# An attention and expert kernel: down products three chunks behind, a third buffer for middle values, other places for loads and last results

## The reference, cut to what matters

```python
x = x + xattn(layernorm(x), ctx, ...)          # x is (8, 256, 256), ctx (8, 77, 256); differential attention, 16 heads
x = x + ffn(layernorm(x), gate_w, gate_up_proj, down_proj)

def ffn(hidden_states, gate_w, gate_up_proj, down_proj):      # E = 8 experts, I = 1024, TOP_K = 2
    x = hidden_states.reshape(-1, H)                          # 2048 tokens x 256
    probs = softmax(x @ gate_w.T)
    w, idx = top_k(probs, TOP_K)
    w = w / sum(w, axis=-1, keepdims=True)
    combine = zeros((T, E)).at[arange(T)[:, None], idx].add(w)
    def step(acc, (gup, dn, ce)):
        g, u = split(x @ gup.T, 2, axis=-1)
        return acc + ce[:, None] * (silu(g) * u @ dn.T)
    return scan(step, zeros_like(x), (gate_up_proj, down_proj, combine.T))
```

## Time and profile before

| | |
|---|---|
| device time, median of 3 runs | 564.85 us (564.73 to 565.91) |
| time of the profiled execution | 568.35 us |
| its span, first to last instruction | 566.5 us |
| TensorE busy (products) | 499.4 us, 88% |
| VectorE, ScalarE, GpSimd busy | 385.6, 339.0, 273.6 us (68%, 60%, 48%) |
| mean granted TensorE clock | 0.946 of 2.4 GHz |
| up products, 1440 | 188.8 us busy |
| down products, 720 | 104.3 us busy |

### The profile page before, as it was taken

The page is one execution under the profiler, slowest core; times in us unless marked ns, Lnnn a source line. Parts: engine busy times, 40 slices in busy tenths (PEclk is TensorE's granted clock), DMA queues, the critical chain, the costliest instruction groups (busy, mean ns, idle before and its releaser), DMA issues.

```text
span 566.5 us, 12111 instructions
## 1 busy us (share of the span) xinstructions
PE 499.4 (88%) x3738; PEld 367.4 (65%) x3756; DVE 385.6 (68%) x805; ACT 339.0 (60%) x642; POOL 273.6 (48%) x347
## 2 busy tenths in 40 slices
PE   4695889999998888689798999999999999999970
PEld 3463556676665655325576888878888888777640
DVE  5337358889887747587577988887676676666551
ACT  1220488889789777275575777765665556554530
POOL 5006454575554544104126565656567566563244
PEclk9986699999999989699899999999999999999985
DMA  6567757768667543463646767866555545563133
GB/s 215 189 162 163 233 144 239 209 190 249 218 170 216 171 132 95 137 200 113 172 103 112 151 131 196 183 116 153 91 104 85 96 76 94 100 71 65 20 32 43
DMA packets 88090, 79.89 MB, mean 141 GB/s; under 512 B 49176, under 2 KB 73368, under 8 KB 87896
## 3 DMA queue, kind: packets, MB, share of 16 engines
q1 hardware_dynamic: 76512, 63.38, 40.7%
q0 software_dynamic: 11520, 15.74, 17.1%
HBM read 49.08 MB, written 22.41 MB: 126 GB/s over the span
## 4 chain that ended last, share of the span: by engine, by line
PE 65%; DMA 9%; DVE 7%; ACT 7%; issue 6%; SPq 2%; POOL 2%; another core or an unknown queue 1%; ACTq 0%; DVEq 0%; POOLq 0%
PE bank L1441 25%; PE bank L1458 12%; PE bank L1270 5%; PE bank L1224 5%; PE bank L1256 4%; DVE FB L1156 2%; PE bank L1293 2%; DVE FB L1160 2%; PE bank L1470 2%; PE bank L1306 2%; PE bank L1238 2%; PE bank L1279 2%; ACT FB L867 2%; DMA x_parts<-WE 2%; PE bank L1318 2%
## 5 line engine op out<-in xcount | busy, mean ns | idle before, releaser
L1441 PE MATMUL bank<-FB,WE 128*128 128x0 bf16 x1440 | 188.8, 281 | 2.7 <-DVE FB L1156 1.0
L1441 PEld LDWEIGHTS bank<-FB,WE 128*128 x1440 | 137.4, 98 | 34.9 <-issue 5.1
L700 POOL DMA_INDIRECT out<-FB,slot_tok x60 | 100.4, 1674 | 97.7 <-DVE FB L1172 93.3
L867 ACT ACTIVATE FB<-FB 128x512 bf16<-128x512 f32 x120 | 75.6, 630 | 71.1 <-DVE FB L1156 63.2
L1160 DVE TENSOR_TENSOR FB<-FB 128x512 bf16<-128x512 f32 x120 | 83.3, 694 | 47.4 <-ACT FB L867 42.2
L1458 PE MATMUL bank<-FB,WE 128*128 128x0 bf16 x720 | 104.3, 281 | 5.3 <-DVE FB L1160 3.3
L1156 DVE TENSOR_TENSOR FB<-FB,bank 128x512 f32<-128x512 f32 x120 | 82.0, 683 | 28.8 <-ACT FB L861 22.3
L691 POOL DMA_INDIRECT FB<-x_parts,slot_tok x60 | 61.2, 1020 | 69.0 <-DVE slot_tok L1124 27.0
L861 ACT ACTIVATE FB<-bank 128x512 f32<-128x512 f32 x120 | 70.6, 588 | 34.0 <-PE bank L1441 28.3
L1458 PEld LDWEIGHTS bank<-FB,WE 128*128 x720 | 68.1, 98 | 23.9 <-issue 8.3
L624 POOL TENSOR_TENSOR WE<-FB,WE 128x256 bf16<-128x256 f32 x104 | 67.9, 679 | 23.0 <-ACT WE L731 23.0
(11 more groups left out here) (180 smaller groups left out, 618.9 us busy)
## 6 DMA issues: line engine op xcount, KB each, us to landing
FB<-w SPq DMA_DIRECT2D x26, 512.0 KB, 5.5
WE<-w SPq DMA_DIRECT2D x44, 256.0 KB
WE<-q_parts SPq DMA_DIRECT2D x32, 200.0 KB
WE<-x SPq DMA_DIRECT2D x16, 256.0 KB, 5.3
q_parts<-FB SPq DMA_DIRECT2D x32, 128.0 KB
x_parts<-WE SPq DMA_DIRECT2D x20, 128.0 KB, 4.3
out<-WE SPq DMA_DIRECT2D x20, 128.0 KB, 5.3
q_parts<-WE SPq DMA_DIRECT2D x16, 128.0 KB
```

Of the source, the lines that this page charges most:

```text
L700: pool.indirect_dma_start(out=out, out_offset=bass.IndirectOffsetOnAxis(ap=slot_tok[:, c:c + 1].bitcast(U32), axis=0), in_=y_sb[c % 2], in ...
L867: nc.scalar.activation(hT[k % 3][:, 0, :], hid[k % 2], ACT.Copy).then_inc(hi_ready, 1)
L1441: ins = nc.tensor.matmul(to, wf[:, bass.ds(at + o, P)], xgT[s % 2][:, 2 * part + kc, :].shape_from_register(long[s % 2]), start=(z == 0), ...
```

## The change

It does these things:

- The down products of a chunk come after the up products of the third chunk behind it (`LAG = 3`), and three, not two, are left after the last up. The results of a slot are turned back after chunk 4 and chunk 7 of the next slot (chunk 5 in the last slot).
- ScalarE does silu(k) before hidden_hi(k - 1), VectorE hidden(k) before hidden_lo(k - 1). In slots 0 to 3 (k < 32) a third buffer, `hid_more`, in the place of weights that come later, joins the two of `hid`, and silu(k) waits for hidden_lo(k - 3).
- The late parts are split at other chunks (`FILL_OF`); the results are scaled at chunks 5, 6 of the next slot and 0, 1 of the one after.
- On SP the loads of late parts of a slot's last two chunks stand behind the first turns of the following slot; the last x load stands before the first four late loads.
- X2 of tile 15 stands before LG of tile 14.
- Of the last eight result tiles the first two go to `y_sb` as before, then two to free parts of `xgT`, two to `xg` and two to `y_sb`; two of the last four turned halves have banks of their own, and a semaphore `y_end` counts four of the last scatters.

```diff
+FILL_OF = ((3, 4, 5, 7), (4,), (2, 3, 4, 7), (2, 3, 4, 7), (1, 2, 3, 4, 5, 6, 7), (1, 2, 3, 4, 5, 6, 7))
...
+LAST = NTP - SUB
+LAG = 3
+THREE = EARLY * FC
...
+        hid_more = tail[:, 2 * W1N - 2 * CAP:2 * W1N].bitcast(F32)
...
+        def hid_of(k):
+
+            return (*hid, hid_more)[k % 3] if k < THREE else hid[k % 2]
+
+        def turned_bank(n):
+
+            return {2 * NS - 3: y_bank(NS - 2, 1), 2 * NS - 1: bank[0]}.get(n, turn_bank)
...
+        def result_tile(c):
+
+            if LAST - 2 <= c < LAST:
+                return xgT[NS % 2][:, c % 2, :].bitcast(F32)
+            return xg[c % 2].bitcast(F32) if LAST <= c < LAST + 2 else y_sb[c % 2]
...
-                if kind == "OO" and TPB * b + i == TT - TPB - 2:
+                if kind == "XD" and b == B - 1:
                     for j in range(LSTG):
                         load_late(j)
...
-                        if FC * s + (0, 3)[half] <= due[j] < FC * s + (3, FC)[half]:
+                        if FC * s + (-2, 3)[half] <= due[j] < FC * s + (3, FC - 2)[half]:
                             load_late(j)
...
                     for p in range(2):
-                        pool.wait_ge(y_out[p], 8 * c)
+                        pool.wait_ge(y_out[p], 8 * c - 16 * (c == LAST))
+                if c == LAST:
+                    pool.wait_ge(y_end, 32)
...
             def silu(k):
                 act.wait_ge(g_mm, k + 1)
-                if k >= 2:
-                    act.wait_ge(lo_ready, k - 1)
-                nc.scalar.activation(hid[k % 2], up_bank[k % 2][0][:, :], ACT.Silu).then_inc(sil_ready, 1)
+                if k >= (3 if k < THREE else 2):
+                    act.wait_ge(lo_ready, k - (2 if k < THREE else 1))
+                nc.scalar.activation(hid_of(k), up_bank[k % 2][0][:, :], ACT.Silu).then_inc(sil_ready, 1)
...
+                    silu(k)
                     if k > 0:
                         hidden_hi(k - 1)
-                    silu(k)
-                    if c in (1, 2) and s > 0:
-                        yT_copy(s - 1, c - 1)
+                    if c in (2, 3) and s > 0:
+                        yT_copy(s - 1, c - 2)
...
-                if c >= 2:
+                if LAST <= c < LAST + 2:
+                    dve.wait_ge(xg_turned[c % 2], 32 * (NS - 1))
+                elif c >= LAST + 2:
+                    dve.wait_ge(y_out[c % 2], 16 * (c // 2 - 2))
+                elif LAST - 2 <= c < LAST:
+                    dve.wait_ge(g_mm, FC * (NS - 1))
+                elif c >= 2:
                     dve.wait_ge(y_out[c % 2], 16 * (c // 2))
...
+                    hidden(k)
                     if k > 0:
                         hidden_lo(k - 1)
-                    hidden(k)
-                    if c in (4, 5, 7) and s > 0:
-                        result(SUB * (s - 1) + (4, 5, 7).index(c))
-                    if c == 0 and s > 1:
-                        result(SUB * (s - 1) - 1)
+                    if c in (5, 6) and 0 < s < NS - 1:
+                        result(SUB * (s - 1) + c - 5)
+                    if c in (0, 1) and s > 1:
+                        result(SUB * (s - 2) + 2 + c)
+                    if c in (5, 6) and s == NS - 1:
+                        result(SUB * (s - 1) + 2 * (c - 5))
+                        result(SUB * (s - 1) + 2 * (c - 5) + 1)
...
-                    if c >= 2:
-                        down(s, c - 2, at[s])
+                    if c >= LAG:
+                        down(s, c - LAG, at[s])
                     elif s > 0:
-                        down(s - 1, FC - 2 + c, at[s - 1])
-                    if c in (3, 6) and s > 0:
-                        turned_result(s - 1, c // 6)
+                        down(s - 1, FC - LAG + c, at[s - 1])
+                    if c == 4 and s > 0:
+                        turned_result(s - 1, 0)
+                    if c == (7 if s < NS - 1 else 5) and s > 0:
+                        turned_result(s - 1, 1)
```

31 lines of the change are left out of this document (17 added, 14 removed).

## The result

The changed kernel takes 559.8 us (median of four runs, 558.9 to 560.6) where the kernel before took 565.4 beside it (564.7 to 568.5): a ratio of 0.989, 95% interval 0.985 to 0.993. It is faster by 5.6 us; the forecast had 16.2 us and a range that ended 5 us short of the time. The profiled execution has a span of 558.5 us in a time of 560.4, against 566.5 us in the earlier trace rows. So the two profiles are 8.0 us apart where the medians are 5.6 us apart: the profiled execution of the kernel before was itself a long one, 568.35 us.

The account below looks back on a forecast made before the run. TensorE, the busiest engine, was taken to bound the kernel, with gapless products from slot 4 on. Terms 2.35 + 9.8 - 0.9 + 0 + 4.9 = 16.15 us took 564.85 to 548.6 us; range 545.5 to 554.5 us.

Parts of the forecast that it names:

- all three stretches: Slots 0 to 3, the end of attention and the tail: where TensorE's products do not follow each other without a gap.
- Part 3: Slots 4 to 13, two hid buffers: ring of 1.96 us stays under TensorE's 2.335; 0 us, bounds -0.5 and +2.
- Part 2: Slots 0 to 3: new order and third buffer open the ring, 9.8 us gained; 0.9 us taken off for late rows.
- Rival A: Slots 1 to 3: turned rows become the bound, lengths stay; 4.2 us less gain, 552.8 us; chance 0.18.
- The one named above all: Sign that the forecast is wrong: the stretches before slot 4 shorten by less than 6 us together.
- the ring: Slots 0 to 3: hidden, hidden_hi, hidden_lo and hops make 1.99 us a chunk, costing 0.43 us where products need 1.56.
- Part 1: End of attention: x sooner (1.70) and two swapped products (0.65) start the expert stage 2.35 us sooner; ends 0 and 3.1.
- Rival C: End of attention and turns: clock stays up after the shorter wait, no turn is late; 546.5 us; chance 0.10.
- Part 4: Tail: one down chunk sooner (0.9 us) and last results in their own homes (4.0 us), together 4.9 us.
- D: Slots 0 to 3: the 1.99 us ring closes again over hT or up banks; 556.5 us; chance 0.04.
- E: Slots 4 to 14: two buffers make one serial ring, 2.58 us a chunk against 2.335; 570 us; chance 0.04.
- B: End of attention: x lands sooner but another transfer or the clock holds; 2.35 us less, 551.0 us; chance 0.12.

Follow-up runs that it names:

- i_res: The changed kernel with plain copies for turns and only the order of the results put back: 553.4 us, ratio 0.987 to the kernel before.
- k_res: The same kernel as i_res (only the order of the results put back), run again on another visit: 554.3 us, ratio 0.984.
- the control: The kernel before with each of its 56 turns replaced by two plain copies of half the bytes, turning left out: 565.5 us, ratio 0.998.
- j_tail_only: The kernel before with plain copies for turns and only the last results in eight homes: 563.7 us, ratio 0.997.
- h_after: The changed kernel with its turns replaced by plain copies, nothing else altered: 560.3 us, ratio 0.991 to the kernel before.
- i_two_buf: The changed kernel with plain copies for turns and without the third middle-value buffer, two in every slot: 564.2 us, ratio 1.002.
- i_late_res: The kernel before with plain copies for turns and a slot's third and fourth result a chunk later: 566.8 us, ratio 1.006.
- k_newwin: The kernel before with plain copies for turns, late weight loads of chunks 6 and 7 moved behind the next slot's first two turns: 566.3 us, ratio 1.004.

## Where the prediction was right and where it failed

**The direction** was right, and so was the reading of all three stretches as chains that this change opens. The size was 2.9 times too large.

**Part 3 failed, and it is the step that decided.** It booked 0 us for slots 4 to 13 with a bound of +2, "if results wait longer for their scatters", and gave as its reason that results fall into VectorE's waits. That is VectorE's view. What the later results move is GpSimd's queue and, through the two gather buffers, the rows of a slot to come. The profile pair has +6.7 us from slot 4 to the last up products. The text had the chain itself, under Part 2: results of chunks 0 and 1, gathers about 9 us into the slot, turns at 12 or 13, landing at 16 or 17. It priced it at 0.9 us for slots 3 and 4, because they were to be 16.6 us long, and dropped it for slots 4 to 7, which took 17.3 to 18.6 us in the kernel before, as if 1 us of slack were enough. At slots 3 and 4 the changed kernel has these times (turns 12.9 and 12.4 us into the slot before) and no wait; for slots 5 to 7 the turns came at 14.1, 14.9 and 15.9 and the rows 4.6 to 5.1 us later where TensorE waited for them, so the chain got longer and was not merely short of slack. With the gathers back by 1 to 2 us the stalls are 1.3 us in i_res and none in k_res, against 4.4, and with the loads back as well slots 4 to 7 have the control's length in all three profiles. Which of the two weighs more the runs do not decide, and they explain the excess of the form with plain copies, 2.8 us. Rival A named the mechanism, and set it in slots 1 to 3 alone; it came in slots 4 to 7. That its price of 4.2 us is near what the results' place gave back (4.6 and 7.4 us in the profiles, 1.5 of them in slot 2; 2.5 and 4 in the time) is chance, since it was added up from slots 1 to 3. Of the signs, gaps at slot starts came, as named for A. The one named above all, less than 6 us gained ahead of slot 4, did not: 9.5 us were gained there (11.1 with the 1.6 us ahead of P1), and the forecast failed behind it.

**Part 3 also left out the loads.** The diff moves SyncE's loads behind turns; the forecast counted that as a help to the turns, and didn't ask who waits for the loads. ScalarE does, 2.6 us at one part, with silu queued behind it. In the profiles it is worth about 2 us in slot 5; in the time it could not be told apart.

**Part 2** forecast 58.6 us for slots 0 to 3 where 62.1 came; 0.9 more had been set aside for late rows. Slot 0 (11.8 forecast, 12.20) and slot 3 (16.6, 16.89) are sized well, and the mechanism holds: without the third buffer slots 0 and 1 are 1.5 and 2.2 us longer. Slot 1 was mis-sized by 1.6 us: the forecast took products and two result turns, but the second turn waits 0.80 us for VectorE's result (the row at 293.18), and there are gaps of 0.4 and 0.2 us in chunks 3 and 6 (283.25 to 285.20, 288.78 to 290.58), whose releaser no row names. With the results put back it still takes 14.7 to 16.0 us, so their place is not the cause; what is stays open. Slot 2 was mis-sized by 1.2: its stall of 1.8 us stands in the kernel before as well, and the forecast took it for part of the ring.

**Part 1** forecast 2.35 us; it is 2.5 to 2.7 over all the profiles. x sooner gave 1.6 (1.70 forecast: P1 of tile 13 to that of tile 15 took 11.4 to 12.1 us in five profiles, and 10.2 in most of those with the edit), the swap 1.15 (0.65: from P1 of tile 15 to the first up 39.4 to 39.6 us before, 38.3 after). Rival C's clock didn't come: TensorE waits 2.35 us in place of 4.31 ahead of the transpose of tile 14, and the granted clock falls all the same, to 0.88 in 230 to 231 us and to 0.50 in 231 to 237, which is 1.2 GHz (before: 0.89 in 231 to 232, then 0.50). The shorter wait did not keep it up. The Trainium skill (TensorE: Matmul & The Clock Gate, What's actually happening) has the clock follow how busy the array has lately been; a fall behind a wait agrees with that, but what the prediction drew from it, that a wait of 2.6 us might leave the clock up, is not borne out by this trace.

**Part 4** forecast 4.9 us, 3.6 came. The term of 0.9 us, a down chunk sooner, is nothing: from the last up to the turn of results are 6.78 us after and 6.70 in j_tail_only, where products stay two chunks behind, so the last hidden value and not the count of open down chunks sets it: ahead of the last down products j_tail_only waits 1.13 us for hidden_lo, the changed kernel 0.34. The rest is 4.0 against 3.6.

**The rivals.** D (slots 0 to 3 don't open) and E (one serial ring) did not come; slots 8 and on take 131.6 and 131.2 us. B did not.

**The sum again**: -2.6 (-3.1 in this pair) for the end of attention, -6.4 for slots 0 to 3, -3.6 for the tail, and +6.7 for what was booked at nothing: 5.9 us, where the timed runs show 5.6. Without the +6.7 it would be 12.6, still 3.6 us short of the forecast, for the sizes of slots 1 and 2 and of the tail.

## What to carry to other kernels

When results move by one chunk, follow what each of them releases through every queue that it passes, up to the buffer that comes free and to the engine that waits for what is loaded there, and write the slack of that chain in us for each slot. Here a chain that was to land within 1 us of its need cost stalls of 0.5 to 3 us, at slots that changed from one profile to the next. Before a load is put behind something "that is waited for more", ask who waits for the load and what is queued behind that engine. Here, putting results and loads back while keeping the buffer, the order of products, the sooner x and the homes at the end gave 0.977 to 0.985 in place of 0.991 (with plain copies for turns; the version with the real turns was not run; slots 4 to 7 cost more in it, so what it would gain is open).

## What the runs showed that I had not expected

- **The same kernel stalls at different slots.** The kernel with both put back had its largest stall at slot 4 (1.95 us), at slot 2 (0.5) and at slot 7 (1.8 us) in three profiles. A profile of one execution shows which chain lacks slack, and not where it will be felt.
- **The clock after a stall.** After the 3.00 us at slot 7 the changed kernel's products ran at half speed (2.78 us for 12, where the next take 1.49; the granted clock is 0.50 in 388 to 391 us). After the 2.49 us at slot 4 of h_after they did not (1.65 us, as in the chunks behind; granted clock 1.00), and after the shorter 1.86 us at slot 6 of the same profile they did (2.80 us; 0.52 in 370 to 373). In i_two_buf 2.08 us were followed by slow products (3.08 us) and 2.31 us by fast ones (1.50). The length of the wait alone doesn't tell.
- **Slot 2's stall seems to belong to the program.** It is in the original kernels and in their forms here with nearly the same slot length (18.20 and 18.28 us before, 17.77 and 17.82 after), and absent from i_res and k_res, which are one kernel (16.25 and 16.27), from all three with both put back (16.2 to 16.3) and from i_late_res and k_newwin (16.6), which differ from the control in other instructions altogether. Its cause was not found.
- **Edits that the profile shows clearly can vanish in the time**: 2.7 us are 0.5% of it, and the intervals of eleven runs are 0.3 to 0.4% to either side. The 2.7 us in the tail lie within that; the 2.7 us at the end of attention do not, so part of them is lost elsewhere.
